# Attention B of a three-block transformer kernel: projections of tiles 2 to 5 issued one step sooner, second maxima sooner, weight dequantising later

## What is computed

```python
def _dequant_matmul(x, qw, scales):
    w = (qw.astype(jnp.float32) - ZERO) * jnp.repeat(scales, GS, axis=0)
    return x @ w
...
q = _apply_rope(q, cos, sin)
k = _apply_rope(k, cos, sin)
k = jnp.repeat(k, rep, axis=1)
v = jnp.repeat(v, rep, axis=1)
scores = jnp.einsum('bhqd,bhkd->bhqk', q, k) / math.sqrt(HD)
scores = jnp.where(causal[None, None], scores, jnp.finfo(scores.dtype).min)
attn = jax.nn.softmax(scores.astype(jnp.float32), axis=-1).astype(q.dtype)
ctx = jnp.einsum('bhqk,bhkd->bhqd', attn, v)
return _dequant_matmul(ctx, qw_o, scales_o)
```

## Time and profile before

| | before |
|---|---|
| median of 3 timed runs | 1569.06 us (1565.88 to 1569.36) |
| the profiled execution, its own time | 1571.05 us |
| its span, first to last instruction | 1569.2 us |
| PE busy | 1469.0 us (94%) |
| DVE busy | 1237.7 us (79%) |
| ACT busy | 868.9 us (55%) |
| POOL busy | 237.6 us (15%) |
| granted TensorE clock, mean of the span | 0.972 |

### The profile page before, as it was taken

The page is one execution under the profiler, slowest core; times in us unless marked ns, Lnnn a source line. Parts: engine busy times, 40 slices in busy tenths (PEclk is TensorE's granted clock), DMA queues, the critical chain, the costliest instruction groups (busy, mean ns, idle before and its releaser), DMA issues.

```text
span 1569.2 us, 23528 instructions
## 1 busy us (share of the span) xinstructions
PE 1469.0 (94%) x7932; PEld 698.8 (45%) x7932; DVE 1237.7 (79%) x2583; ACT 868.9 (55%) x1468; POOL 237.6 (15%) x174
## 2 busy tenths in 40 slices
PE   5779999999999997899999999998999999999988
PEld 3412333333333354455555555554555555555534
DVE  4288888888886388787897887887887888878873
ACT  2205767676778324565665665664665665646630
POOL 2002000000000132221212212212212212211020
PEclk9957999999999998999999999999999999999989
DMA  3894000000000233566576575675684674653621
GB/s 97 150 143 134 1 1 0 0 0 0 0 0 11 64 94 98 105 140 144 121 137 139 120 150 127 129 147 120 128 160 111 141 145 110 134 96 67 115 54 54
DMA packets 352234, 144.64 MB, mean 92 GB/s; under 512 B 314680, under 2 KB 324408, under 8 KB 352128
## 3 DMA queue, kind: packets, MB, share of 16 engines
q1 hardware_dynamic: 352144, 143.48, 43.8%
HBM read 59.64 MB, written 6.19 MB: 42 GB/s over the span
## 4 chain that ended last, share of the span: by engine, by line
PE 73%; DVE 14%; ACT 6%; DMA 3%; issue 3%; SPq 0%; POOL 0%; DVEq 0%; ACTq 0%
PE ps L1433 9%; PE ps L1215 9%; PE ps L1435 9%; PE ps L1434 9%; PE ps L1268 7%; PE ps L1254 7%; PE ps L1395 4%; PE ps L1514 3%; PE ps L1516 3%; PE ps L1515 3%; ACT hl L680 2%; DVE hl L1038 2%; PE ps L1358 2%; DMA scratch<-pieces 2%; PE ps L1458 2%
## 5 line engine op out<-in xcount | busy, mean ns | idle before, releaser
L672 ACT ACTIVATE x<-ps,nmb,factor 128x128 f32<-128x128 f32 (+7 forms) x256 | 211.6, 832 | 290.9 <-DVE nmb L1023 290.9
L823 DVE TENSOR_REDUCE mx<-ps 128x1 f32<-128x512 f32 x512 | 326.4, 686 | 52.8 <-PE ps L1215 49.4
L581 ACT ACTIVATE proj<-ps 128x1024 f32<-128x1024 f32 x256 | 248.4, 1021 | 105.7 <-PE ps L1254 104.8
L1215 PE MATMUL ps<-ks,qs 96*128 (+1 forms) x512 | 200.1, 414 | 16.3 <-DVE mx L823 8.5
L1038 DVE SCALAR_TENSOR_TENSOR hl<-x,rden,hl 128x128 f16<-128x128 f32 (+7 forms) x256 | 208.3, 814 | 4.6 <-ACT hl L680 4.3
L680 ACT ACTIVATE hl<-x,rden 128x128 f16<-128x128 f32 (+7 forms) x256 | 184.1, 767 | 23.2 <-DVE rden L1034 22.5
L1021 DVE TENSOR_REDUCE nmr<-ps 128x1 f32<-128x128 f32 (+7 forms) x256 | 191.9, 750 | 0.0
L500 POOL TENSOR_TENSOR tmp<-tmp 128x640 f32<-128x640 f32 x64 | 98.4, 1538 | 532.1 <-DVE tmp L1017 532.1
L1433 PE MATMUL ps<-wh,xTh 128*128 128x256 f16 (+1 forms) x512 | 167.6, 327 | 0.0
L1434 PE MATMUL ps<-wl,xTh 128*128 128x256 f16 (+1 forms) x512 | 167.5, 327 | 0.0
L1435 PE MATMUL ps<-wh,xTl 128*128 128x256 f16 (+1 forms) x512 | 167.4, 327 | 0.0
(11 more groups left out here) (155 smaller groups left out, 2149.6 us busy)
## 6 DMA issues: line engine op xcount, KB each, us to landing
scale<-sp_n SPq DMA_DIRECT2D x32, 384.0 KB, 4.3
st<-in_L_attn_b_qw_q_dram SPq DMA_DIRECT2D x32, 256.0 KB, 2.8
st<-in_L_attn_b_qw_o_dram SPq DMA_DIRECT2D x32, 256.0 KB, 3.0
scale<-so_n SPq DMA_DIRECT2D x32, 256.0 KB, 3.6
qs<-scratch SPq DMA_DIRECT2D x24, 256.0 KB, 8.4
hlT<-hl SPq DMA_TRANSPOSE x256, 3.5
scratch<-pieces SPq DMA_DIRECT2D x5, 768.0 KB, 13.4
xnat<-attn_a_hidden_state_dram SPq DMA_DIRECT2D x8, 256.0 KB, 4.8
```

Of the source, the lines that this page charges most:

```text
L581: nc.scalar.activation(pbuf[:, e % 4, :].rearrange("p (b n) -> p b n", b=2), ps[:, b:b + 2, :], ACT.Exp, scale=float(HD) ** -0.5).then_inc ...
L672: nc.scalar.activation(pr[:, h, 0:n], flat(2 * (h % 2), n), ACT.Exp, bias=nmb[:, h:h + 1], scale=factor[:, par, 0:1], accum_out=den[:, h:h ...
L823: nc.vector.tensor_reduce(mx[:, f, k // 2, k % 2:k % 2 + 1], ps[:, bank(k), :], AX.X, ALU.max).then_inc(s_mx, 1)
L1215: mm(ps[:, bank, :], qs[0:STACK, ds(g * R + h, 1), f * HALF + qt * P:f * HALF + (qt + 1) * P], ks[0:STACK, ds(g, 1), kh * HALF:(kh + 1) * ...
```

## The change

The projections of tiles 2 to 5 are issued one step sooner, at the end of PE's step: after `values` of step `t` PE now projects tile `t + 2`, for `t` from 0 to 3. In steps 1 to 4 nothing is projected between the scores of heads 0 and 1 any more. Steps 0, 5, 6 and 7 keep it there. Banks 6 and 7 may then be full with the tile after the next when the next tile is turned, so the turned queries and key of tiles 1 to 4 go to banks 1 and 3 (`turned_banks`), which the short scores of steps 0 to 3 leave free. DVE takes the second maximum in front of the rotation in steps 0 to 4 and dequantises there after `turned`; in step 0 it also takes `low` of head 3 ahead of the first maximum. ACT rounds the chunk after the exponentials of head 3 in all steps. No instruction is added or taken away.

```diff
--- before.py
+++ after.py
@@ -217,6 +217,10 @@
         def v_slot(t, par):
 
             return t if t > 1 else t + T * par
+
+        def turned_banks(t):
+
+            return (1, 3) if 1 <= t <= T // 2 else (6, 7)
 
         def k_slot(t, par):
 
@@ -642,10 +646,10 @@
 
             def turned(v, t, par):
                 act.wait_ge(s_qkT, v + 1)
-                nc.scalar.activation(qTh[:, t % 2].rearrange("p h n -> p (h n)"), ps[:, 6, :], ACT.Copy,
+                nc.scalar.activation(qTh[:, t % 2].rearrange("p h n -> p (h n)"), ps[:, turned_banks(t)[0], :], ACT.Copy,
                                      scale=HEADROOM / (XSCALE * WSCALE)).then_inc(s_qke, 1)
                 c = k_slot(t, par) * P
-                nc.scalar.activation(kTh[:, c:c + P], ps[:, 7, 0:P], ACT.Copy,
+                nc.scalar.activation(kTh[:, c:c + P], ps[:, turned_banks(t)[1], 0:P], ACT.Copy,
                                      scale=HEADROOM / (XSCALE * WSCALE)).then_inc(s_qke, 1)
 
             def context_high(g, t):
@@ -686,12 +690,12 @@
                     values(u + 1, par if t < T - 1 else 1 - par, t2)
                 high(0)
                 high(1)
-                if not last:
-                    high_part(g + 1, t, 1 - par)
                 if not end:
                     turned(u + 1, t2, par if t < T - 1 else 1 - par)
                 exponentials(2)
                 exponentials(3)
+                if not last:
+                    high_part(g + 1, t, 1 - par)
                 if exists(*before(g, t, 1)):
                     context_high(*before(g, t, 1))
                 high(2)
@@ -1041,11 +1045,11 @@
             def turned(v, t, par):
 
                 dve.wait_ge(s_qke, v * 2 + 2)
-                nc.vector.scalar_tensor_tensor(qTl[:, t % 2].rearrange("p h n -> p (h n)"), ps[:, 6, :],
+                nc.vector.scalar_tensor_tensor(qTl[:, t % 2].rearrange("p h n -> p (h n)"), ps[:, turned_banks(t)[0], :],
                                                HEADROOM / (XSCALE * WSCALE), qTh[:, t % 2].rearrange("p h n -> p (h n)"),
                                                ALU.mult, ALU.subtract).then_inc(s_ql, 1)
                 c = slice(k_slot(t, par) * P, (k_slot(t, par) + 1) * P)
-                nc.vector.scalar_tensor_tensor(kTl[:, c], ps[:, 7, 0:P], HEADROOM / (XSCALE * WSCALE), kTh[:, c],
+                nc.vector.scalar_tensor_tensor(kTl[:, c], ps[:, turned_banks(t)[1], 0:P], HEADROOM / (XSCALE * WSCALE), kTh[:, c],
                                                ALU.mult, ALU.subtract).then_inc(s_ql, 1)
 
             def add(v, t, par):
@@ -1073,17 +1077,23 @@
                 one, two = before(g, t, 1), before(g, t, 2)
                 if exists(*one):
                     low(u - 1, 2, (one[1] + 1) * P)
+                if exists(*one) and t == 0:
+                    low(u - 1, 3, S)
                 if t == 0:
                     dve.wait_ge(s_fcr, g + 1)
                 maximum(u, 0, n, par)
-                if exists(*one):
+                if exists(*one) and t > 0:
                     low(u - 1, 3, (one[1] + 1) * P)
-                if not last:
+                sooner = t <= T // 2
+                if sooner:
+                    maximum(u, 1, n, par)
+                elif not last:
                     dequantise(g + 1, t)
                 if not end:
                     rope_cos(u + 1, t2)
                     rope_sin(t2)
-                maximum(u, 1, n, par)
+                if not sooner:
+                    maximum(u, 1, n, par)
                 invert(u, 0)
                 if not end:
                     values_low(u + 1, par if t < T - 1 else 1 - par, t2)
@@ -1094,6 +1104,8 @@
                     turned(u + 1, t2, par if t < T - 1 else 1 - par)
                 else:
                     final_statistics(0, 1)
+                if sooner and not last:
+                    dequantise(g + 1, t)
                 low(u, 1, n)
                 invert(u, 1)
                 if exists(*two):
@@ -1450,11 +1462,12 @@
                 project(v, t, 1, par)
                 project(v, t, 0, par).then_inc(s_pj, 1)
 
-            def turn_b(v):
+            def turn_b(v, t):
                 pe.wait_ge(s_rpa, v + 1)
                 pe.wait_ge(s_vl, v + 1)
                 for h in range(BH):
-                    dst = ps[:, 6, h * P:(h + 1) * P] if h < R else ps[:, 7, 0:P]
+                    q, k = turned_banks(t)
+                    dst = ps[:, q, h * P:(h + 1) * P] if h < R else ps[:, k, 0:P]
                     ins = nc.tensor.transpose(dst, rc1[:, h * P:(h + 1) * P], ident[:])
                 ins.then_inc(s_qkT, 1)
 
@@ -1524,7 +1537,7 @@
                 one, two = before(g, t, 1), before(g, t, 2)
                 pe.wait_ge(s_ql, u * 2 + 2)
                 keys(g, t, 0, par)
-                if not end:
+                if not end and (t == 0 or t > T // 2):
                     project_all(u + 1, *after(g, t), par if t < T - 1 else 1 - par)
                 keys(g, t, 1, par)
                 if exists(*two):
@@ -1534,13 +1547,15 @@
                     output_second(*two, par if t >= 2 else 1 - par)
                 keys(g, t, 3, par)
                 if not end:
-                    turn_b(u + 1)
+                    turn_b(u + 1, after(g, t)[1])
                 if exists(*one):
                     values(*one, par if t >= 1 else 1 - par)
+                if t < T // 2:
+                    project_all(u + 2, g, t + 2, par)
 
             project_all(0, 0, 0, 0)
             tokens(2, 4, 5)
-            turn_b(0)
+            turn_b(0, 0)
             tokens(2, 6, 7)
             steps(step)
             output_first(G - 1, T - 2, (G - 1) % 2)
```

## The result

The changed kernel takes 1581.46 us (median of 6 runs, 1577.75 to 1583.03). The kernel before takes 1568.54 us (6 runs, 1565.88 to 1569.39). The ratio is 1.008, with a 95% interval of 1.0064 to 1.0096: slower. The profiled execution of the changed kernel took 1577.79 us, with a span of 1576.0 us against 1569.2 before.

The account below looks back on a forecast made before the run. PE was taken as the bound. Six middle groups at +1.20 us (7.2), the last 1.2 and the first 0 gave +8.4 on the profiled 1571.05, 1579.5; the median lying 2.0 lower, 1578, range 1568 to 1589.

Parts of the forecast that it names:

- The waits that go: In front of steps 2 to 4, PE's waits for `kTl` (1.58, 1.01, 0.34 us) were to go altogether.
- The waits that come: At the turning in steps 1 to 4, PE was to wait 1.33, 1.25, 1.17 and 1.06 us for `rope_add`.
- the last handover: From POOL's `rope_add` to PE's turning, taken as 0.2 us, as read between PE and DVE.
- The meeting on DVE and POOL: Rival, 0.17 together with a lower clock: POOL delays `low` or `invert` on DVE, +1.0 us a group, about 1586.
- The sum of a group: Steps 1 to 4 were to change by -0.67, +0.09, +0.69 and +1.09 us, together +1.20.
- Step 0: Turning some 0.8 us sooner, but SP's transposes gate `values`: 0 taken, bounds 0 and -1.1 us.
- nothing measurable: Rival, 0.20: time within 0.3%, step 0 giving 1.1 us, so 0.1 us a group, 1570.
- The clock: Rival, in the same 0.17: waits around step 0's turning lower the clock, 2.8 us lost seven times, 19 us, 1597.
- a sign of being wrong: Listed among signs against the forecast: a clock below 1.00 in a middle group.
- The whole: Six middle groups 7.2 us, the last 1.2, the first 0 (bounds -3 and +1.2): +8.4 us.
- the same 1.2: Last group, with no chunk to dequantise and smaller old waits: at least 1.2 us more, as in a middle group.

Follow-up runs that it names:

- e4: Changed kernel with the late dequantise put in front of `turned` instead of behind it: 1581.81 us, ratio 1.0051.
- e3: Changed kernel with DVE's order in step 0 alone put back as before the change: 1579.79 us, ratio 1.0051.
- e5: Changed kernel with `low` of head 3 ahead of the first maximum in steps 1 to 4 too: 1568.26 us, ratio 0.9992.
- e8: e7 with the first half of tile 2's projection between the turning and `values` in step 0: 1554.62 us, ratio 0.9895.
- e9: e6 with half of tile 2's projection between the turning and `values` in step 0, without e7's edit: 1551.24 us, ratio 0.9889.
- e1: Changed kernel with the chunk's dequantise and rounding back in their early places, projection and second maximum still moved: 1603.87 us, ratio 1.0204.
- e2: Changed kernel with all projections back between the scores of heads 0 and 1, DVE and ACT as changed: 1579.26 us, ratio 1.0058.
- e7: e6 with `values` ahead of the turning on PE in steps 1 to 3: 1568.3 us, ratio 0.999.
- e6: Changed kernel with the edits of e4 and e5 together: 1561.33 us, ratio 0.9945.

## Why the prediction was right, and where its terms were off

**1. The waits that go.** Right: no wait for `kTl` is left, in any group. One reading was too large: the 6.9 us of waits for transposes before the change were not those of step 0, for 5.1 of them are the one wait at the end of attention B. What the prediction made of step 0 doesn't rest on that sum.

**2. The waits that come.** Right in mechanism and place, a little too large. Against the step's start, the turning was to begin at 5.45, 6.01, 6.57 and 7.14 us in steps 1 to 4. It began at 5.29, 6.12, 6.41 and 6.99. The term that was off is the last handover: I took 0.2 us from POOL to PE, by analogy with PE to DVE. The chain above shows 0.04 (967.53 to 967.57). This alone explains the -0.16, -0.16 and -0.15 of steps 1, 3 and 4. The idle times in the brackets are another 0.16 smaller, since they count from the end of the last scores and I counted from the issue: in step 1 PE is free to issue at 966.40 and the turning begins 1.17 later, where the row says 1.01. Counted from the issue the waits were 1.17, 1.06, 0.90 and 0.73 us, for the 1.33, 1.25, 1.17 and 1.06 of the prediction: from step 2 on PE also arrives 0.29, 0.11 and 0.18 later than I had it, since it stands for a moment in front of head 2's scores (in step 2 from 975.11 to 975.39). That alone shortens the wait and doesn't move the turning.

**3. The meeting on DVE and POOL.** I gave it 0.17, together with the clock, as a rival of 1.0 us a group. The meeting is real. It costs PE time in one place, and about a quarter of that. The timelines of DVE and POOL where step 2 begins:

```profile
972.93 0.88 DVE L1042 SCALAR_TENSOR_TENSOR hl<-x,rden,hl 128x256 f16<-128x256 f32 x1
973.74 0.55 DVE L1025 TENSOR_REDUCE nmr<-ps 128x1 f32<-128x384 f32 x1
...
974.45 0.48 DVE L1042 SCALAR_TENSOR_TENSOR hl<-x,rden,hl 128x256 f16<-128x256 f32 x1
```

```profile
971.88 1.65 POOL L509 TENSOR_TENSOR wl<-st,wh 128x768 f16<-128x768 f32 x1 [4.36 <-ACT wh L604]
```

A `low` of the same shape takes 0.88 us while POOL works and 0.48 when POOL is done. `rope_add` stretches it as well, in each of steps 0 to 2, behind the chain where PE doesn't wait for it (here in step 1):

```profile
967.04 0.76 DVE L1042 SCALAR_TENSOR_TENSOR hl<-x,rden,hl 128x256 f16<-128x256 f32 x1
```

```profile
965.98 1.54 POOL L504 TENSOR_TENSOR tmp<-tmp 128x640 f32<-128x640 f32 x1 [8.67 <-DVE tmp L1021]
```

Both times `low` ends 0.28 us after POOL does (973.81 and 973.53, 967.80 and 967.52): it looks as if it did its work only once POOL was through. The `low` of head 2 is stretched in steps 2 and 3 too (1.01 and 1.05 us), but there the first maximum is not late. The first maximum of step 2 starts 973.74 - 972.72 = 1.02 us into the step, where I had 0.75: 0.27 late. That is why step 2 alone was longer than I said (11.92 against 11.79), and e4, by which this `low` starts sooner, gave 0.27 us a group back. The Trainium skill (GPSIMD Engine Reference, Key points) says that POOL contends with DVE instructions that have two SBUF inputs. These rows agree, `low` being such an instruction.

**4. The sum of a group.** Predicted for steps 1 to 4: -0.67, +0.09, +0.69, +1.09, thus +1.20. Measured: -0.81, +0.22, +0.55, +0.95, thus +0.91. The difference of 0.29 is four handovers that I took too long by 0.16, less the 0.27 of the meeting and 0.02 a step for the turning, which takes 0.60 (968.17 - 967.57) where I had 0.58. Step 0 was to give nothing, since SP's transposes gate `values`. Its turning starts 951.36 - 942.86 = 8.50 us into the step for 9.42 before, 0.92 sooner where I had 0.8. But `values` starts 953.20 - 942.86 = 10.34 us into it, where it was 844.31 - 834.01 = 10.30, and e3 shows the edits of step 0 to be worth 0.01 us. The 1.1 us that the rival "nothing measurable" would have taken from there are not there.

**5. The clock.** I had it as part of a rival: 2.8 us in each of seven groups, "against it" the 1.00 of all middle groups. It happened in two of seven in the profiled execution, one of them a middle group, which I had named as a sign of being wrong. Three windows of the changed kernel, each soon after the turning of step 0 (columns as in the earlier trace rows):

```profile
952.00:957.00 5.00, 3.93 (x20) 1.78 (x19) 2.91 (x7) 2.49 (x7) 1.33 (x1) 1.00 0.97 196
1064.00:1069.00 5.00, 3.66 (x11) 1.39 (x12) 2.91 (x7) 2.49 (x7) 1.46 (x1) 0.66 0.87 208
...
1402.00:1407.00 5.00, 3.87 (x12) 1.50 (x13) 2.04 (x6) 1.29 (x6) 0.00 (x0) 0.66 0.18 38
```

In the second of these the matmuls of `values` follow one another at 0.43 us, where 0.22 is usual (timeline of PE):

```profile
1065.34 0.58 PE L1527 MATMUL ps<-hlT,vh 128*128 128x512 f16 x1 [1.35 <-DMA hlT<-hl]
1065.72 0.63 PE L1528 MATMUL ps<-hlT,vl 128*128 128x512 f16 x1
1066.15 0.63 PE L1529 MATMUL ps<-hlT,vh 128*128 128x512 f16 x1
...
1068.27 0.38 PE L1528 MATMUL ps<-hlT,vl 128*128 128x512 f16 x1
1068.49 0.38 PE L1529 MATMUL ps<-hlT,vh 128*128 128x512 f16 x1
```

This is the lower of the two levels, 1.2 GHz. Ahead of it PE stood 0.95 us at the turning, worked 0.6, and stood 1.35. From the turning of step 0 to that of step 1 it takes 17.91 - 16.21 = 1.70 us more than in the group before. Of that 0.27 are transposes that land later (`values` starts 2.11 us after the turning for 1.84), and 1.43 are the clock. The same sum gives 1.5 for the fall of the last group. In e5, where the transposes land as in the group at full clock, a fall costs 1.7. In the profiled execution of the kernel before, no group but the first has one. The Trainium skill (TensorE: Matmul & The Clock Gate, What's actually happening) says that the throttled state is the default and activity releases it. The rows agree in so far as e8 and e9, which put work into this idle place, show no fall behind the first group; but neither does the kernel before, whose step 0 has 1.02 and 0.69 us of idle time.

**6. The whole.** I compare the profiled executions between the turnings of step 7, so that each group keeps its own step 0, begin with the first turning of all, ahead of step 0 of the first group, and end with the last one. The first group takes 0.9 us more (I took 0). The six middle ones take 7.2 more, and 5.8 without the one fall of 1.4 among them, where I had 7.2, for the reasons of points 2 to 4. The last takes 4.0 more, and 2.5 without its fall of 1.5, where I had 1.2. That is 12.1, and without the falls 9.2, against the 8.4 predicted. So the sum is near in part by luck, since errors cancel in it: 1.4 too much in the middle groups, 2.2 too little in the first and the last. Of the last group I wrote that its old waits are smaller and then still took "the same 1.2". Before the change its steps, with no chunk to dequantise, were 1.3 us shorter (35.67 us from the turning of step 1 to that of step 4, against 36.97 in a middle group), and the new waits come there as elsewhere; its `values` in step 0 also starts 0.5 us later than before.

The part ahead of that first turning, which the change doesn't touch, took 4.7 us less in the profiled execution (606.14 for 610.83), and the part behind the last turning 0.6 less. So the spans differ by 6.8 us only. The medians differ by 12.9, which is 4.5 more than the forecast's 8.4. The clock, a term that the forecast put at nothing, took 2.9 of it in the profiled execution; that one is 3.7 us quicker than the median, so what the clock took in the others isn't known from it.

What stays open is what decides in which group the clock falls. The length of the idle place in step 0 bears on it. In the last group the wait in front of `values` is longest, 1.45 to 1.55 us in the changed kernel and in e1, e2 and e4 to e7, and in all seven the clock fell there. It did not fall there in the kernel before and in e3, where 0.69 and about 1.0 us of idle time stand around the turning, nor in e8 and e9, where the place is filled. In the other groups no such order shows: the second group of e5 kept its clock with a wait of 1.56 us, e3 has the step 0 of the kernel before and two falls, the kernel before has none, e5 has four beside that of the last group. Only one execution of each kernel has a trace. For the others the mean clock of the whole execution is on record, and the long ones have the lower one: in e2 the five of 1576.9 to 1578.0 us had 0.969 to 0.971, those of 1580.5 to 1582.9 had 0.965, and that of 1589.1 had 0.961. The kernel before does the same: of 25 executions beside e1 to e4, the 21 below 1575 us had 0.971 to 0.976, the four from 1578.8 to 1582.7 had 0.964 to 0.970. So a lower clock goes with much of the scatter, in the kernel before too. In which part of the span it fell there is not shown, and filling the wait did not end the scatter (e8 7.3 us over four executions, e6 without the filling 1.0).

## What to carry to other kernels

When work on the bounding engine is moved to cover a late result, ask what it covered where it stood: write out the chain that was behind it, piece by piece from the rows, and compare its end with the engine's new arrival. The waits that go and the waits that come are then a sum like any other, here right within 0.3 us a middle group. Repair the chain itself (e5 took one `low` out of it, e4 moved a dequantise that made its first piece late), then fill a wait with work that waits for nothing (e9's half projection). Moving the cover once more, as in e7, only moves the wait.

## What the runs showed of the hardware that I had not expected

- An idle place of 0.95 and 1.35 us around 0.6 us of work was in one group followed by a stretch at half the clock. In e2, e4 and e7 the same group, with 0.95 and 1.36 to 1.38 us, kept its clock. A fall cost 1.4 to 1.7 us. Over the kernels there were between none and five such groups of seven.
- A `low` of 128x256 took 0.48 us alone and 0.88 us beside POOL's low part of the chunk, 0.76 beside `rope_add`, and ended 0.28 us after POOL both times. `rope_add`, which also has both its inputs in SBUF, was not stretched in turn: 1.54 us in the changed kernel as before.
- POOL hands over to PE in 0.04 us (POOL's end to the start of the turning), a fifth of what I had read between PE and DVE.
